# Decoder layer on one core: the first stage's row normalisation on ScalarE, its offset on GpSimd

## What is computed

```python
x = x + _L0_attn_ref(_layernorm(x, axis=-1), L0_attn_ln_gamma, L0_attn_ln_beta, ...)

def _L0_attn_ref(x, ln_gamma, ln_beta, q_gamma, k_gamma, w_q, w_k, w_v, w_o, b_o):
    xn = _layernorm(x, ln_gamma, ln_beta)      # (x - mean) / sqrt(var + eps) * gamma + beta
    q, k, v = proj(w_q), proj(w_k), proj(w_v)
    qn = _rmsnorm(q, q_gamma) * dh ** (-0.5)
    kn = _rmsnorm(k, k_gamma)
    ...
```

## Time and profile before

| | |
|---|---|
| median of 3 runs | 2232.93 us (2232.64 to 2234.2) |
| the profiled execution, its own time | 2231.65 us |
| its span | 2229.9 us |
| PE busy | 2131.5 us, 96% of the span |
| DVE busy | 1666.7 us, 75% |
| ACT busy | 1555.7 us, 70% |
| POOL busy | 1384.8 us, 62% |
| granted PE clock, mean | 0.991 of full speed |
| first stage, batch 1 of 2 | from about 26 to 156 us |
| first stage, batch 2 of 2 | from about 1131 to 1262 us |

### The profile page before, as it was taken

One profiled execution on the slowest core, in us unless ns is written; L12 is line 12 of the kernel. 1 busy time (PEld: TensorE's weight loads), 2 busy tenths in 40 slices (PEclk: granted clock), 3 DMA queues, 4 the chain that ended last, 5 costly groups with the idle time before them and its releaser, 6 DMA issues. The chain is left out here.

```text
span 2229.9 us, 50857 instructions
## 1 busy us (share of the span) xinstructions
PE 2131.5 (96%) x19320; PEld 1210.9 (54%) x19320; DVE 1666.7 (75%) x2889; ACT 1555.7 (70%) x1763; POOL 1384.8 (62%) x982
## 2 busy tenths in 40 slices
PE   6999999999998899899999999999999988998999
PEld 3544666666665455444445456666666654554444
DVE  6998888888888666753379988888888885677522
ACT  4556999999997566631145589999999965666210
POOL 3425989898992586630234169989898826866210
PEclk9999999999999999999999999999999998999999
DMA  4210000000003102102122100000000030020000
GB/s 114 62 43 1 11 2 11 11 11 11 11 11 89 40 1 49 39 31 65 43 62 63 33 1 11 11 2 11 11 11 11 11 97 32 1 68 20 20 24 34
DMA packets 102422, 66.43 MB, mean 30 GB/s; under 512 B 75346, under 2 KB 75346, under 8 KB 102226
## 3 DMA queue, kind: packets, MB, share of 16 engines
q1 hardware_dynamic: 102226, 63.57, 12.8%
HBM read 46.69 MB, written 8.39 MB: 25 GB/s over the span
## 5 line engine op out<-in xcount | busy, mean ns | idle before, releaser
L627 POOL TENSOR_TENSOR qkn<-wide 128x1024 f16<-128x1024 f32 x420 | 883.9, 2133 | 113.0 <-PE bank L753 98.6
L967 DVE TENSOR_REDUCE sq<-bank 128x1 f32<-128x512 f32 x1024 | 676.2, 684 | 137.0 <-PE bank L696 132.7
L887 ACT ACTIVATE wide<-bank,shift 128x1024 f32<-128x1024 f32 x512 | 569.1, 1115 | 34.9 <-POOL qkn L627 15.6
L874 ACT ACTIVATE wide<-bank,shift 128x1024 f16<-128x1024 f32 x444 | 492.4, 1109 | 11.0 <-PE bank L712 7.8
L711 PE MATMUL bank<-q_hh,ko 128*128 128x512 f16 x1024 | 389.1, 380 | 7.4 <-ACT wide L887 7.1
L696 PE MATMUL bank<-ko,q_hh 128*128 128x512 f16 x1024 | 386.6, 379 | 8.9 <-DVE sq L967 6.7
L712 PE MATMUL bank<-q_lm,k_h 65*128 65x512 f16 x1024 | 389.0, 380 | 0.0
L735 PEld LDWEIGHTS bank<-v_hl,wide 128*128 128x128 f16 x4096 | 274.4, 97 | 122.0 <-DVE wide L1034 8.7
L735 PE MATMUL bank<-v_hl,wide 128*128 128x130 f16 (+1 forms) x4096 | 303.2, 212 | 5.2 <-DVE wide L1034 4.4
L753 PEld LDWEIGHTS bank<-v_hl,qkn 128*128 128x128 f16 x4096 | 189.0, 97 | 60.7 <-DVE qkn L1038 3.9
L753 PE MATMUL bank<-v_hl,qkn 128*128 128x65 f16 x4096 | 206.6, 193 | 3.5 <-DVE qkn L1038 3.5
(11 more groups left out here) (231 smaller groups left out, 4314.0 us busy)
## 6 DMA issues: line engine op xcount, KB each, us to landing
wide<-in_x SPq DMA_DIRECT2D x32, 256.0 KB, 2.7
q_lm<-in_x SPq DMA_DIRECT2D x32, 256.0 KB, 3.2
ko<-in_L_ffn_W SPq DMA_DIRECT2D x32, 256.0 KB, 4.1
q_hh<-q_hh SPq DMA_DIRECT2D x32, 128.0 KB, 2.6
ko<-k_h SPq DMA_DIRECT2D x32, 128.0 KB, 2.8
out<-bo_b SPq DMA_DIRECT2D x16, 256.0 KB, 2.0
out<-xbo_b SPq DMA_DIRECT2D x16, 256.0 KB, 2.0
q_lm<-sq SPq DMA_DIRECT2D x248, 0.2 KB, 4.8
```

The costliest lines, as they stand in the source:

```text
L627: pool.tensor_tensor(probs_l[:, p % 2, :], probs[:, p % 2, :], probs_h[:, p % 4, :], ALU.subtract).then_inc(pl_pool, 1)
L874: act.activation(probs_h[:, p % 4, :], SB[p % 2][:, :], ACT.Exp, bias=shift[:, 0:1])\
L887: act.activation(probs[:, p % 2, :], SB[p % 2][:, :], ACT.Exp, bias=shift[:, 0:1]).then_inc(p_ready, 1)
L967: dve.tensor_reduce(pm[:, s, k:k + 1], MB[k % 2], AX_X, ALU.max).then_inc(mx_free, 1)
```

## The change

Tiles 2 to 15 of each batch are normalised by ACT instead of DVE. POOL makes, after the scale, an offset -mean * scale (one more instruction on one column, with a wait for its own scale before it), and ACT computes scale * x + offset in one activation (`Identity`, with both as per-row operands). In ACT's step it stands between `row_high` of tile t + 1 and the second `square`. The wait for the transposes of the slot's last tile moves with it. DVE's step loses one instruction. Tiles 0 and 1 stay on DVE.

```diff
-        rows_rs = sb(top, "rs_a", [P, 2, 2], F32)
+        rows_rs = sb(top, "rs_a", [P, 3, 2], F32)
...
+        a_nb = sem("a_nb")
...
-        def row_normalise(dve, b, t, s, first=False):
+        def row_offset(pool, b, t, s):
+
+            pool.wait_ge(a_rs, b * KB + t + 1)
+            pool.nop(nofuse=True)
+            pool.tensor_scalar(rows_rs[:, 2, s:s + 1], rows_mv[:, s, 0:1], rows_rs[:, 1, s:s + 1], -1.0, ALU.mult, ALU.mult)\
+                .then_inc(a_nb, 1)
+
+        def row_normalise_scalar(act, b, t, s):
+            T0 = b * KB
+            act.wait_ge(a_nb, b * (KB - 2) + t - 1)
+
+            act.wait_ge(a_t_done, T0 + t - 1)
+            act.activation(rows_n[:, s, :], rows_in[:, s, :], ACT.Identity, bias=rows_rs[:, 2, s:s + 1],
+                           scale=rows_rs[:, 1, s:s + 1]).then_inc(a_y, 1)
+
+        def row_normalise(dve, b, t, s):
             T0 = b * KB
             dve.wait_ge(a_rs, T0 + t + 1)
-            if not first:
-
-                dve.wait_ge(a_t_done, T0 + t - 1)
             dve.tensor_scalar(rows_n[:, s, :], rows_in[:, s, :], rows_mv[:, s, 0:1], rows_rs[:, 1, s:s + 1],
                               ALU.subtract, ALU.mult).then_inc(a_y, 1)
...
                             if next2:
                                 row_scale(pool, b, t + 2, s)
+                                row_offset(pool, b, t + 2, s)
                                 row_affine(pool, b, t + 2, s)
...
                             if next1:
                                 row_high(act, b, t + 1, turned(t + 1)[0])
+                            if next2:
+                                row_normalise_scalar(act, b, t + 2, s)
                             square(t, 1, KBK[s], a_k_done)
...
                             if next1:
                                 row_low(dve, b, t + 1, *turned(t + 1))
-                            if next2:
-                                row_normalise(dve, b, t + 2, s)
                             sum_squares(t, 1)
```

More of the change, by code:

```diff
@@ L425, in _ @@
                 row_stats(dve, 0, 0, 0)
-                row_normalise(dve, 0, 0, 0, first=True)
+                row_normalise(dve, 0, 0, 0)
                 split_low(dve, 0, PIECES_P1[:1], stage1, *wq_of)
@@ L430, in _ @@
                 split_low(dve, 0, PIECES_P1[1:2], stage1, *wq_of)
-                row_normalise(dve, 0, 1, 1, first=True)
+                row_normalise(dve, 0, 1, 1)
                 dve.wait_ge(s_pool, 4)
@@ L2663, in _ @@
                                             row_stats(dve, b + 1, j, j)
-                                            row_normalise(dve, b + 1, j, j, first=True)
+                                            row_normalise(dve, b + 1, j, j)
                                         else:
```

## The result

| | before | with the change |
|---|---|---|
| median | 2233.35 us (4 runs) | 2264.02 us (4 runs) |
| profiled execution, its own time | 2231.65 us | 2263.59 us |
| its span | 2229.9 us | 2261.8 us |

The ratio is 1.014, 95% interval 1.0126 to 1.0154: slower by 30.7 us, by the two medians. The prediction said 2266.5 (2252 to 2275). One of the four runs with the change took 5618.34 us, for a cause that isn't known; the ratio leaves it out, while the median of the table counts it (the other three have 2263.72 us, 30.4 us more than before).

A forecast was written before the change was run, and what follows sets the result against it. PE and DVE were taken to bound the first stage together. Batches of 16.7 and 17.4 us sum to 34.1, less half a microsecond: +33.6 us, a median of 2266.5 us, range 2252 to 2275.

The forecast's parts named there:

- The chain: First stage, steps with a normalisation: loop of statistics, scale, offset, activation, square, sum, heads, scaling becomes 1.28 us longer each.
- The first steps: Steps 0 to 2: existing gaps absorb part, leaving 0.76, 0.55, 1.28 us (first batch) and 1.28, 1.28, 0.78 (second).
- The half microsecond: First stage, both batches: taken off the 34.1 us sum for unnamed timeline gaps of 0.05 to 0.2 us.
- Rival 1: Activation fits into ACT's 2.90 us gap, leaving PE the only bound: 5 us faster, about 2228 us; chance 0.04.
- Rival 2: End of the first stage: PE does late values while DVE catches up, so no change, 2233 us; chance 0.03.
- Rival 3: First stage: PE, less busy, is granted a lower clock; 6 to 11 us more, 2272 to 2278 us; chance 0.06.
- Rival 4: ACT's `Identity` needs other tables, two loads a step: 72 us more, about 2338 us; chance 0.01.

## Why the prediction was right

*The chain, 1.28 us a step.* Measured 1.25. From the second sum of step 2 to that of step 13 it was 45.60 to 135.99 before and is 46.94 to 151.10 now: 104.16 - 90.39 = 13.8 us in eleven steps, against 14.1 predicted. Its parts: activation 0.81 us, as in the earlier trace rows; hold 0.72; own wait 0.18; offset 0.26; hand-over 0.04. The three instructions of the later stage were the right price list. Three steps of DVE take 28.6 us (statistics of steps 5 and 8 at 71.81 and 100.44), predicted 28.8, and PE waits for 13.7 us in the twelve steps of the four stretches, 3.4 for three, predicted 3.5. The small miss in the chain is the square behind the activation, which took 0.58 us instead of 0.60, and DVE's pick-up of 0.03 instead of 0.04.

*Late data, not a busy engine.* The run with every second tile and the run without the offset show that the loss follows the time of the chain; the runs with early statistics show that ACT's 0.72 us and POOL's offset cost nothing measurable outside it. All of these came out within what the chain had them expected at; only the run behind the heads did not, in its size and in where the second square stands.

*The first steps* were the mis-sized term: 2.6 us in the first batch and 3.3 in the second, by the gaps of the earlier trace rows. In the first batch the sum of step 2 moved from 45.60 to 46.94, 1.3 us, and this stage had begun 0.5 us earlier in the profiled run (statistics at 25.81, not 26.32), so it had grown by 1.9 us. In the second batch that sum moved from 1150.77 to 1168.17, of which 14.98 had come with the start of the stage: 2.4 us. What the prediction missed is in the timeline of DVE before, outside the waits for other engines that it went by:

```profile
43.73 0.18 DVE L329 BATCH_NORM_AGGREGATE mv_a<-st_a 128x2 f32<-128x6 f32 x1 [0.54 <-DVE st_a L326]
...
1136.75 0.76 DVE L918 TENSOR_SCALAR rp<-ms 128x16 f32<-128x16 f32 x1
```

The aggregate of step 2 in the first batch waited 0.54 us for its own statistics, and in the second batch the first instruction of the scaling in step 0 took 0.76 us, where it takes 0.16 with the change. Neither came again in the profiled run with the change, so that part of the 1.28 us was offset. Why they were longer before stays open.

Together the two stages grew by 32.0 us, against a sum of 34.1: about 1.7 us less in the first steps, and 0.7 less in the 22 steps behind them, where the chain is 1.25 us instead of 1.28. The half microsecond that the prediction took off for unnamed gaps brought its 33.6 nearer to the 31.9 of the profiled execution, for another reason than the one it gave. Against the 30.7 between the medians it is 2.9 us too high.

*Rival 1* (it fits into the gap, faster) was rightly small: it needed the offset 1.5 us earlier. The early statistics brought that, and then its mechanism held, but its gain of 5 us did not show: 2.3 us between the medians, within the noise.

*Rival 2* (taken back at the end of the stage): the last sum of step 13 is 15.1 us later than before (135.99 to 151.10) and the cast behind the stage 15.2 us, so nothing was taken back. Of this shift 15.0 us are still there at the start of the second batch (1132.18 to 1147.16).

*Rival 3* (the clock): did not come in the changed kernel, whose stretches all have 1.00. It did in the run with the activation behind the heads, where PE waited more than twice as long at a time. Its price was reckoned wrongly: a mean clock of 0.94 makes 25 us of PE 25 / 0.94 = 26.6 us, not 28. The forecast itself does not use this price; only the upper end of the range, 2275, leans on it.

*Rival 4* (table loads): none came; ACT's timeline has the activation at 83.38 and the square at 84.10 with nothing between.

On the rule of Perfetto Trace Analysis (Trainium skill), "Optimizing Scalar/DVE Operations", that a saturated DVE may hand work to Scalar: here DVE was saturated in the stage and Scalar was not, and the hand-over cost 1.4%. It became harmless only when the operands were early, and brought nothing that could be measured, since PE was the bound beside DVE.

## To carry to other kernels

An idle share says how much work an engine could take, not when. Before moving an instruction into a gap, look at when its last operand is ready against when the instruction behind it must start: here the gap of 2.9 us lay wholly before the operand, and an in-order queue turned the wait for it into a delay of the whole loop. If the gap is at the wrong time, move the producer first; and where two engines bound a stage together, relieving one gives no more than what the other has idle (here 2.0 of 99 us).

## What the runs showed that was not expected

With the activation behind the heads, the granted clock fell in a stage that was at 1.00 throughout before the change and with it. In a stretch of 14 us it had a mean of 0.76, with PE busy for 10.55 of them, and a step took 13 us instead of 10.2. The length of PE's wait alone does not explain it. The wait of 3.45 us (3.44 in two rows) comes in twelve steps of the two batches. In six of them, as in the row at 81.88 above, the transposes behind the wait took 0.65 or 0.66 us; in the other six they took 1.11 or 1.12 us, and the clock was at its lower level, 1.2 GHz:

```profile
132.68 1.12 PE L380 MATMUL bank<-ident,wide 128*128 128x128 f32 x4 [3.44 <-POOL wide L371]
```

In the changed kernel PE was busy for 23.09 of 28 us (0.82) in one stretch, no wait of PE inside the stage was longer than 1.4 us, and the clock stayed at 1.00. So the delay of the changed kernel cost only itself. What exactly made the clock fall in the other run was not tested.
